# Attention 1 of a decoder: the causal mask and the row extremum in one VectorE instruction per head, no mask matmuls

## What is computed

```python
B, S, D = x.shape
H, dk = (NUM_HEADS, D_K)
q = jnp.einsum('bsd,hkd->bhsk', x, wq.reshape(H, dk, D))
k = jnp.einsum('bsd,hkd->bhsk', x, wk.reshape(H, dk, D))
v = jnp.einsum('bsd,hkd->bhsk', x, wv.reshape(H, dk, D))
sin, cos = _rope_tables(S, dk, THETA, x.dtype)
q = _apply_rope(q, sin, cos)
k = _apply_rope(k, sin, cos)
scores = jnp.einsum('bhqk,bhsk->bhqs', q, k) / jnp.sqrt(jnp.asarray(dk, x.dtype))
causal = jnp.triu(jnp.ones((S, S), dtype=bool), k=1)
scores = jnp.where(causal, -jnp.inf, scores)
attn = jax.nn.softmax(scores, axis=-1)
out = jnp.einsum('bhqs,bhsv->bqhv', attn, v).reshape(B, S, H * dk)
return jnp.einsum('bsf,df->bsd', out, wo)
```

## Time and profile before

| | |
|---|---|
| median of 3 runs | 891.43 us (890.92 to 892.2) |
| profiled execution | 891.15 us, span 889.1 us |
| busy: PE, DVE, ACT, POOL | 867.5, 619.0, 433.2, 98.1 us |
| first row maximum of attention 1 starts | 322.86 us |
| last row maximum of attention 1 starts | 398.03 us |
| TensorE clock granted, 322.86 to 399.97 us | 1.00 |

### The profile page before, as it was taken

How to read it: one execution, slowest core, us unless ns; L and a number is a source line. 1 busy time by engine, 2 the same in 40 slices (tenths; PEclk the granted TensorE clock), 3 DMA queues, 4 the chain that set the end, 5 groups by cost and what they waited for, 6 DMA issues and landing times.

```text
span 889.1 us, 13931 instructions
## 1 busy us (share of the span) xinstructions
PE 867.5 (98%) x5281; PEld 667.9 (75%) x5281; DVE 619.0 (70%) x1154; ACT 433.2 (49%) x1081; POOL 98.1 (11%) x79
## 2 busy tenths in 40 slices
PE   8998999999999999999999999999999999999998
PEld 5665778888888786667767777777667788888886
DVE  4669756566665767666888888889866666666565
ACT  8554634333433459884344444445466444344342
POOL 4001000000000141000322323223200000000000
PEclk9998999999999999999999999999999999999999
DMA  6003111111100330003200000000210111111001
GB/s 193 1 2 127 36 38 51 53 53 45 44 0 1 125 130 2 2 16 142 112 1 1 1 2 1 1 1 1 93 52 3 52 39 51 53 53 35 18 1 47
DMA packets 12535, 37.33 MB, mean 42 GB/s; under 512 B 2080, under 2 KB 4352, under 8 KB 11712
## 3 DMA queue, kind: packets, MB, share of 16 engines
q1 hardware_dynamic: 12448, 36.58, 12.6%
q0 software_dynamic: 32, 0.01, 0.0%
HBM read 35.54 MB, written 1.05 MB: 41 GB/s over the span
## 4 chain that ended last, share of the span: by engine, by line
PE 86%; DVE 7%; ACT 5%; issue 1%; POOL 0%; DMA 0%; DVEq 0%; ACTq 0%; POOLq 0%
PE ps L1458 79%; PE ps L2104 3%; PE ps L1631 2%; DVE P L595 1%; ACT Q L1216 1%; DVE probs_q L940 1%; ACT DT L1033 1%; ACT probs_q L1348 1%; DVE rope_buf L874 1%; DVE stats L519 0%; PE ps L1836 0%; DVE neg_max L930 0%; ACT h_hi L1261 0%; DVE xn L527 0%; DVE weighted_h L745 0%
## 5 line engine op out<-in xcount | busy, mean ns | idle before, releaser
L1261 ACT ACTIVATE h_hi<-weighted_h 128x512 fp32r<-128x512 f32 x100 | 63.2, 632 | 149.1 <-DVE weighted_h L745 147.0
L755 DVE TENSOR_TENSOR h_lo<-weighted_h,h_hi 128x512 fp32r<-128x512 f32 x100 | 69.2, 692 | 66.1 <-ACT h_hi L1261 65.9
L1458 PE MATMUL ps<-xT_second,whi 128*128 128x512 f32 x376 | 108.6, 391 | 1.4 <-ACT silu_g L1256 1.4
L1458 PE MATMUL ps<-xT_first,whi 128*128 128x512 f32 x376 | 109.7, 392 | 0.0
L782 DVE TENSOR_TENSOR shared_gate<-silu_g,row_shares 128x512 f32<-128x512 f32 x88 | 60.9, 692 | 61.9 <-ACT silu_g L1256 61.6
L1256 ACT ACTIVATE silu_g<-ps 128x512 f32<-128x512 f32 x100 | 59.7, 598 | 73.4 <-PE ps L1458 73.3
L1458 PEld LDWEIGHTS ps<-xT_second,whi 128*128 128x128 f32 x376 | 70.0, 188 | 16.9 <-issue 2.5
L1458 PEld LDWEIGHTS ps<-xT_first,whi 128*128 128x128 f32 x376 | 70.0, 188 | 15.9 <-issue 1.5
L1348 ACT ACTIVATE probs_q<-ps,neg_max 128x256 f32<-128x256 f32 x128 | 58.7, 486 | 47.0 <-DVE neg_max L930 47.0
L1458 PE MATMUL ps<-h_hi,wlo 128*128 128x512 f32 x200 | 78.0, 390 | 0.0
L1458 PE MATMUL ps<-h_hi,whi 128*128 128x512 f32 x188 | 74.0, 394 | 0.4 <-DVE h_lo L755 0.3
(11 more groups left out here) (213 smaller groups left out, 1653.4 us busy)
## 6 DMA issues: line engine op xcount, KB each, us to landing
raw<-in_ffn SPq DMA_DIRECT2D x50, 384.0 KB, 3.0
wx<-in_wx SPq DMA_DIRECT2D x4, 2112.0 KB, 7.9
cx<-in_cx SPq DMA_DIRECT2D x1, 1536.0 KB, 6.5
X<-in_x SPq DMA_DIRECT2D x4, 256.0 KB, 6.4
kvc<-in_kvc SPq DMA_DIRECT2D x1, 1024.0 KB, 14.3
out<-X SPq DMA_DIRECT2D x4, 256.0 KB, 2.2
wqkv<-in_wqkv SPq DMA_DIRECT2D x1, 768.0 KB, 7.8
wqkv<-in_wqkv SPq DMA_DIRECT2D x1, 512.0 KB, 5.7
```

Of the source, the lines that this page charges most:

```text
L755: v.tensor_tensor(h_lo[:, u % 2, :], weighted_h[:, u % 2, :], h_hi[:, u % 2, :].bitcast(F32), ALU.subtract).then_inc(act_lo[l], 1)
L1261: a.activation(h_hi[:, u % 2, :], weighted_h[:, u % 2, :], ACT.Copy).then_inc(act_hi[l], 1)
L1458: return pe.matmul(o, l, r, start=start, stop=stop, skip_group_check=True)
```

## The change

The masks leave PE. DVE keeps the mask in SBUF as fp32 (128 columns of zeros, then the 128 columns of neg_qs), made just before the loop. `row_max(n)` becomes one tensor_tensor_reduce for each head and bank: it reads the scores from PSUM and the mask from SBUF, writes -(score + mask) to Q, and gives the minimum of what it wrote, the negated maximum, as accumulator output to nm. It counts `max_done` twice a step, once for each bank. ACT's exponentials read Q in place of PSUM, with scale -1, and write back to Q; they begin when the first bank's half is done. PE's scores open their own accumulation and wait only for `max_done` of step n-2, since nobody but DVE reads the scores. nm has three slots, and `row_max(n)` also waits until PE has turned the exponentials of step n-3 out of Q. A spacer keeps the addresses of the tiles behind identb and negqs. Nothing is changed outside attention 1 but the two casts in attention 0.

```diff
@@ -102,8 +102,7 @@
         rstd = sb("rstd", [P, TILES])
         epsc = sb("epsc", [P, 1])
         eps4 = sb("eps4", [P, 1])
-        identb = sb("identb", [P, 128], BF16)
-        negqs = sb("negqs", [P, 128], BF16)
+        sb("below_wqkv0", [P, 128])
 
         def k(name):
             a, b = CONST[name]
@@ -155,11 +154,12 @@
                 zeros = sb("zeros", [P, 512], BF16, c=layer0)
                 ld_bc = sb("ld_bc", [P, HEADS], c=layer0)
             with ExitStack() as layer1:
-                nm = sb("nm", [P, 2, 8], c=layer1)
+                nm = sb("nm", [P, 3, 8], c=layer1)
                 psum_q = sb("psum_q", [P, 2, 32], c=layer1)
                 prec_q = sb("prec_q", [P, 32], c=layer1)
                 prec_r = sb("prec_r", [P, 32, HD], c=layer1)
                 Q = sb("Q", [P, 3, 2, 512], c=layer1)
+                mask = sb("mask", [P, 2 * 128], c=layer1)
 
         phase = ExitStack()
         with phase:
@@ -600,9 +600,15 @@
             def row_max(n):
 
                 v.wait_ge(pe_s, STEPS + n + 1)
-                heads = 4 if n % 3 == 0 else 2
-                v.tensor_reduce(nm[:, n % 2, 0:2 * heads].rearrange("p (i h) -> p i h", h=heads), step_scores(n).rearrange("p i (h s) -> p i h s", h=heads),
-                                AX, ALU.max, negate=True).then_inc(max_done, 1)
+                if n >= 3:
+                    v.wait_ge(pe_tb, n - 2)
+                heads, width = (4, 128) if n % 3 == 0 else (2, 256)
+                for i in range(2):
+                    for h in range(heads):
+                        columns = slice(width * h, width * h + width)
+                        last = v.tensor_tensor_reduce(Q[:, n % 3, i, columns], step_scores(n)[:, i, columns], mask[:, 256 - width:256], -1.0, 3e38,
+                                                      ALU.add, ALU.min, nm[:, n % 3, heads * i + h:heads * i + h + 1])
+                    last.then_inc(max_done, 1)
 
             def copy_transposed(n):
 
@@ -635,9 +641,6 @@
                         gated_values(b)
                     decayed(a, 1)
                     if a == 0:
-                        v.wait_ge(const_loaded, 16)
-                        v.tensor_copy(identb[:, :], ident).then_inc(setup_v, 1)
-                        v.tensor_copy(negqs[:, :], neg_qs).then_inc(setup_v, 1)
                         normalise(0, 3)
                     if a == NB - 1:
                         normalise(2, a - 3)
@@ -693,6 +696,10 @@
                 for b in range(NB - 1):
                     for j in range(2):
                         project1(b, j)
+                v.wait_ge(const_loaded, 16)
+                v.memset(mask[:, 0:128], 0.0).then_inc(setup_v, 1)
+                v.tensor_copy(mask[:, 128:256], neg_qs).then_inc(setup_v, 1)
+                v.wait_ge(setup_v, 2)
                 for n in range(STEPS):
                     turn, k = divmod(n, 3)
                     b = turn // 2 - 1
@@ -1205,16 +1212,16 @@
             def probabilities(n):
 
                 b, half, k = n // 6, n // 3 % 2, n % 3
-                a.wait_ge(max_done, n + 1)
                 if n % 6 == 0 and b >= 2:
                     a.wait_ge(rec_ready, NB + b - 1)
                 heads, width = (4, 128) if k == 0 else (2, 256)
                 for i in range(2):
+                    a.wait_ge(max_done, 2 * n + i + 1)
                     for h in range(heads):
                         m, e = divmod(h, 2) if k == 0 else (k - 1, h)
                         at = (0 if k == 0 else 16) + 8 * m + 2 * (2 * half + i) + e
-                        last = a.activation(Q[:, n % 3, i, width * h:width * h + width], step_scores(n)[:, i, width * h:width * h + width], ACT.Exp,
-                                            bias=nm[:, n % 2, heads * i + h:heads * i + h + 1], accum_out=psum_q[:, b % 2, at:at + 1])
+                        last = a.activation(Q[:, n % 3, i, width * h:width * h + width], Q[:, n % 3, i, width * h:width * h + width], ACT.Exp, scale=-1.0,
+                                            bias=nm[:, n % 3, heads * i + h:heads * i + h + 1], accum_out=psum_q[:, b % 2, at:at + 1])
                 last.then_inc(p_done, 1)
 
             def copy_transposed(n):
@@ -1600,20 +1607,18 @@
 
                 b, half, k = n // 6, n // 3 % 2, n % 3
                 if n >= 2:
-                    pe.wait_ge(p_done, STEPS + n - 1)
+                    pe.wait_ge(max_done, 2 * (n - 1))
                 heads = 4 if k == 0 else 2
                 by_head = step_scores(n).rearrange("p i (h s) -> p i h s", h=heads)
-                for i in range(2):
-                    mm(by_head[:, i] if k == 0 else by_head[:, i, :, 128:256], identb[:, :], negqs[:, :].unsqueeze(1).to_broadcast([P, heads, 128]), True, False)
                 for h in range(heads):
                     m, e = divmod(h, 2) if k == 0 else (k - 1, h)
                     kk = (kE, kO)[e]
                     for i in range(2):
                         r = slice(64 * half + 32 * i, 64 * half + 32 * i + 32)
                         if k == 0:
-                            last = mm(by_head[:, i, h, :], qT[r, b, m, 0:128], kk[r, b, m, 0:128], False, True)
+                            last = mm(by_head[:, i, h, :], qT[r, b, m, 0:128], kk[r, b, m, 0:128], True, True)
                         else:
-                            last = mm(by_head[:, i, h, :], qT[r, b, m, 128:256], kk[r, b, m, :], False, True)
+                            last = mm(by_head[:, i, h, :], qT[r, b, m, 128:256], kk[r, b, m, :], True, True)
                 last.then_inc(pe_s, 1)
 
             def transposed_probabilities(n):
@@ -1772,7 +1777,6 @@
                             query_or_key(b, j)
                     if 1 <= b < NB - 1:
                         turned(b - 1)
-                pe.wait_ge(setup_v, 2)
                 for n in range(STEPS):
                     turn, k = divmod(n, 3)
                     b = turn // 2 - 1
```

## The result

The change took 888.52 us, the median of 13 runs (886.83 to 890.4), the kernel before 890.67 us in the 13 runs beside them (889.94 to 892.2): a ratio of 0.9979, 95% interval 0.9972 to 0.9986, 1.9 us less. The interval leaves out 1, so the gain is clear of the noise, but it is only just past the 0.2% that the forecast counted as no change. The profiled execution took 888.5 us, its span 886.7 (before 891.15 and 889.1).

A forecast was written before the change was run, and what follows sets the result against it. PE's queue was taken as the bound, then ACT, then DVE. Over four stretches of attention 1's score loop, -0.2 - 1.4 + 0.1 + 1.1 = -0.4 us from 891.43 gave 891.0 us, range 888.5 to 898.0.

The forecast's parts named there:

- r: Cost of DVE's accumulator write behind each tensor_tensor_reduce, the two forming a pair; taken as 0.09 us, bounds 0.07 and 0.17.
- rival A: Cheap accumulator on DVE: r is 0.07, so -2.2 us, 889.2 us; chance 0.27.
- (1): First nine steps of attention 1's score loop: DVE becomes full, the stretch lasts as before but starts sooner; -0.2 us.
- (2): Next seven steps, from row maximum of step 9 to 16: chain alternates DVE and PE, 22.4 us for 23.79; -1.4 us.
- (3): Row maximum of step 16 to that of step 22: DVE 9.25 plus PE 11.22, 20.5 us for 20.37; +0.1 us.
- (4): Row maximum of step 22 to PE's first transposes of it: DVE alone, 6.3 us for 5.22; +1.1 us.
- Rival B: DVE becomes the bound because pairs do not overlap, r = 0.17: +7.0 us, 898.4 us; chance 0.32.
- rival C: The new DVE instruction runs below a column a cycle; at half rate some 18 us more, 909 us; chance 0.03.
- The chain through DVE's copies: PE's transposes wait for DVE's copy queued behind a row maximum; from copy's start to PE's start 0.83 us.
- 92 pairs on the chain: 48 + 20 + 16 + 8 of 128 pairs set the time: change is -0.4 + 92 x (r - 0.09) us.
- ACT hidden: ACT's exponentials from SBUF cost some 0.03 us more each, 25.9 of 27.73 us in the first stretch, adding no time.
- I count nothing: PE's scores wait for maxima of step n-2, earlier than its exponentials; counted as no gain.

The follow-up runs named there:

- experiment 9: The change with a reduction over 64 mask columns behind each pair: 899.72 us, ratio 1.0102; beside it the unedited change again, 888.32 us, ratio 0.9969.
- experiment 10: The change with the 64-column reduction behind each pair, plus filler matmuls in PE's longest waits (steps 7, 12, 18, end): 896.76 us, ratio 1.0066.
- experiment 4: The change with useless filler matmuls in two of PE's waits, 3 in step 7 and 4 behind the last scores: 887.24 us, ratio 0.997.
- experiment 1: The change with the mask matmuls put back on PE ahead of the scores, which overwrite them: 893.05 us, ratio 1.0026.
- experiment 6: The change with PE's scores waiting again for the exponentials of step n-2 instead of its row maxima: 889.48 us, ratio 0.9995.
- experiment 2: The kernel before without its mask matmuls and nothing in their place, so attention 1 isn't causal: 886.09 us, ratio 0.9947.
- experiment 3: The change with DVE's copy moved between the two halves of the row maximum in steps with k = 0 or 2: 890.39 us, ratio 0.9987.
- kernel 8: The change with statistics of X moved later and filler matmuls in steps 7, 12, 18 and at the end: 885.92 us, ratio 0.995.

## Why the prediction was right, and where it was wrong

The forecast was 891.0 us and no change within 0.2%; it came to 888.5, just past 0.2% faster, at the low edge of the range. The forecast time came true by luck. With the r that was measured its own sum gives -7.8 us, 883.6, below the range; what the other terms missed, together 5.5 us the other way, brought it back, and it lies 0.02 us above the range's low end. (The forecast counted from 891.43, the median of 3 runs; that of 13 is 890.67.) Its time is near that of rival A (889.2), but not by A's sum: r was far below A's 0.07, and other things took back what that was worth. In microseconds against the kernel before, the start put with the first stretch:

| | forecast, r = 0.09 | its sum at r = 0.01 | measured |
|---|---|---|---|
| (1) | -0.2 | -4.0 | -1.0 |
| (2) | -1.4 | -3.0 | -1.9 |
| (3) | +0.1 | -1.2 | -0.9 |
| (4) | +1.1 | +0.5 | +0.55 |
| behind | 0 | 0 | +1.0 |
| sum | -0.4 | -7.8 | -2.3 |

Of the measured -1.0 in the first row 0.25 stood there before the loop and isn't the change's.

**What DVE gets: mis-sized, the step that failed first.** r was taken at 0.09 us from ACT's accumulator read, with 0.07 and 0.17 as ends; it is 0.01, under both. The lower end was MATCH_VALUE_LOAD, with the next one 0.07 behind it: a start to start among small instructions isn't the price behind a wide one, where 0.08 us of work starts together with the next instruction. DVE's new work is 64 x 0.345 + 64 x 0.21 - 27.4 = 8.1 us, not 18.1. Beyond its columns the whole pair carries 0.345 - 0.269 = 0.076 us. The Trainium skill (Vector Engine (DVE) Microarchitecture Reference, Measured stream behaviour on trn2) gives about 75 ns an instruction, which I had counted twice; the trace agrees only if the pair counts as one. Rival B's ground, that the next operation waits for an empty pipe, falls with the pairs: a start each 0.345 us at 0.42 us of length. So does rival C: from 128 to 256 columns a pair grows by 0.135 us, the adds' 1.05 ns a column.

**The chain through DVE's copies: right, where it is the chain.** Stretches (3) and (4) come out within 0.3 us of the sum once r is put right, and in experiments 9 and 10 all but the first do within 0.5 (the first is 0.9 and 2.1 us over, each time with a fall of the clock in it). The chain of waits after shows (3) as it was forecast (DVE to 379.3, then PE's pieces):

```profile
379.45 1.06 PE ps L1636 x8
...
381.67 1.06 PE ps L1465 x8
382.73 1.02 PE ps L1636 x8
383.75 2.09 PE ps L1465 x32
385.85 1.02 PE ps L1636 x8
386.87 4.01 PE ps L1465 x32
```

DVE has 8.05 us there for the forecast's 9.25 (16 pairs x 0.08 = 1.3 less), PE 11.45 for 11.22: scores without masks take 1.06 us, not 1.31 - 0.32 = 0.99. The forecast said that it would be wrong if this stretch shrank by 1 us while r is 0.09; it shrank by 0.9 at r = 0.01, which is what the chain asks for.

**92 pairs on the chain: only near r = 0.09.** With cheap pairs DVE's queue at steps 9 and 11 no longer holds PE: in the chain after, PE has 346 to 357 us without a break, and only step 12's eight pairs are left of the 20 in stretch (2), which gives 1.9 us where the sum at r = 0.01 says 3.0. A straight line through one estimate of r overstates what a lower one gives.

**"ACT hidden": wrong in the first stretch.** The extra was sized rightly: four exponentials of 256 columns take 1.96 us on the chain for 1.82, eight of 128 take 3.07 for 2.80, about 0.035 us each. But it isn't hidden. I read stretch (1) by busy shares (PE 26.86 of 27.73, ACT 24.28) and never read its chain. That one shows, before:

```profile
338.80 0.60 ACT P L1225
339.39 1.82 ACT Q L1216 x8
...
342.19 2.80 ACT Q L1216 x16
...
345.48 1.82 ACT Q L1216 x8
347.31 0.50 ACT qk L1196
```

ACT already set the last 9 us of the stretch. In the change's second profile and in experiment 4's it holds the chain for 18 us. The forecast had taken DVE to be full there, which isn't far off (the tie of experiment 4), but a cheaper r then frees DVE and not ACT: little of the 3.8 us that the sum gives back for it can come. The forecast named "ACT is what PE waits for" as what would prove it wrong, and here it did, by masks that come off PE to no use: (1) gains 0.5 us besides its earlier start, and experiment 1 finds 0.9 us there of masks that took PE 3.5 (six at 0.32 and three at 0.53).

**"I count nothing" for the earlier bank release: wrong by 1.0 us** of the chain (experiment 6), in stretches (2) and (3), where the scores would wait for exponentials.

**"PE's clock I leave alone": wrong.** The reason given was that the end kept 1.00 with PE busy 3.97 of 5.22 us, and that PE would stay above that share on average. On average it did in the first three stretches; in the end it is 3.64 of 5.77, because the forecast's own term (4) makes PE wait longer for DVE there, and the fall came behind 1.64 us of work in 3.37. The masks' leaving isn't needed for it: experiment 1 has them all and falls, and experiment 2, with DVE's old work and no masks, falls as well; the first has the longer wait, the second less work beside it. What decides whether a given gap brings a fall stays open: the same gap brought one in one execution and not in another. The end's fall cost 1.0 us in the profiled execution and 2.4 in the second; the one in stretch (1) cost nothing, since the chain over ACT ends at 347 us anyway. In experiment 9 fillers gave 3 us back (experiment 10).

**The predicted waits.** DVE's wait for PE was to fall under 10 us and fell to 12.9; PE was to wait 9 us for DVE's copies and waits 5.8. A DVE with 10 us less to do than forecast would wait more and be waited for less.

## What to carry to other kernels

Price a small instruction behind a wide one by the start of what follows, in the kernel itself or in a kernel of its own, before building a sum on it: here a factor of nine in r was worth 7.4 us in a sum that came to 0.4. Where a stretch has two engines above 85% busy, read its chain before calling one of them hidden. And when work is taken off PE, look at the waits that open in it: statistics moved out of the queue in front of the copies, and a few matmuls in the gaps, gave 2.6 us more than the change itself, 1.6 of them by the statistics alone. A filler that outlasts the wait stands on the chain itself, as the two of step 18 did.

## What the runs showed of the hardware

- DVE's accumulator read starts together with the next main instruction and adds 0.01 us to a pair; a memset of one column adds 0.01 as well, a reduction of 64 columns 0.13.
- The granted TensorE clock fell to half behind stretches in which PE had worked 1.64 of 3.37 us and 2.08 of 3.46, and in a second profile of the same kernel it stayed at 1.00 behind the same 2.08 of 3.46. The kernel before kept 1.00 behind 1.72 of 3.41. Eight records of transposes went from 1.1 to 1.94 us. It didn't fall where fillers had made these 3.27 and 3.40 of 3.40.
- The falls lasted 3.4 or 6.8 us. At the end of the loop they cost 1.0 to 1.5 us when short and 2.4 when long (from the first transposes of step 22 to the addition: 11.33 to 11.87 and 12.76 us for 10.34).
- Times differ from run to run of one kernel with the mean clock: 886.5 us at 1.00 and 890.8 at 0.993 with fillers, 884.9 at 0.998 and 891.4 at 0.992 in experiment 3. Fillers in some of the waits don't end that: experiment 4 spreads over 4.3 us in 12 runs, the change over 3.6 in 13; kernel 8 over 1.0, but in 5 runs.
- ACT takes about 0.035 us longer for an exponential from SBUF (in place, with scale -1) than from PSUM (scale 1), at 256 columns and at 128.
